# Middle stage of a fused vision-tower kernel: the order of the parts of a step rewritten on TensorE, ScalarE, VectorE and SyncE

## What is computed

```python
h = tokens(x)
h = h + attn_L0(layernorm(h))       # distances to 256 fixed positions, softmax
h = h + ffn_L0(layernorm(h))        # matmul with fp8-quantised operands
h = h + attn_L1(layernorm(h))       # softmax(h h^T / sqrt(512)) h within an image
h = h + moe_L1(layernorm(h))        # top 6 of 64 experts + shared experts
```

## Time and profile before

| what | us |
| --- | --- |
| median of 3 runs (4627.1 to 4649.3) | 4639.25 |
| the profiled execution, its own time | 4668.67 |
| its span, first to last instruction | 4666.8 |
| TensorE busy in the span | 2796.7 |
| VectorE busy | 2238.7 |
| ScalarE busy | 1579.3 |
| GpSimd busy | 2460.1 |

### The profile page before, as it was taken

How to read it: one execution, slowest core, us unless ns; L and a number is a source line. 1 busy time by engine, 2 the same in 40 slices (tenths; PEclk the granted TensorE clock), 3 DMA queues, 4 the chain that set the end, 5 groups by cost and what they waited for, 6 DMA issues and landing times. The chain is left out here.

```text
span 4666.8 us, 63125 instructions
## 1 busy us (share of the span) xinstructions
PE 2796.7 (60%) x14076; PEld 2117.4 (45%) x14077; DVE 2238.7 (48%) x7761; ACT 1579.3 (34%) x4281; POOL 2460.1 (53%) x2518
## 2 busy tenths in 40 slices
PE   5888856455545445455454336666666657677663
PEld 4777733233223222232232225655565556566563
DVE  6999965454434444344354333333333333365564
ACT  5777743232222222232222102222222222222221
POOL 5777713445544545435445535555555555565653
PEclk8999965555555555555555557777777776766676
DMA  7777711121221212211112123333333323377774
GB/s 268 248 246 245 245 32 57 61 66 63 67 63 58 63 60 64 65 58 62 61 62 66 61 57 92 94 90 91 84 84 81 84 81 84 106 228 242 237 236 166
DMA packets 401889, 522.45 MB, mean 112 GB/s; under 512 B 65596, under 2 KB 329490, under 8 KB 390514
## 3 DMA queue, kind: packets, MB, share of 16 engines
q1 hardware_dynamic: 318546, 373.60, 26.7%
q0 software_dynamic: 83232, 147.75, 9.3%
HBM read 257.02 MB, written 264.08 MB: 112 GB/s over the span
## 5 line engine op out<-in xcount | busy, mean ns | idle before, releaser
L1089 POOL DMA_INDIRECT xed<-xr,idxs x1014 | 985.9, 972 | 1098.6 <-DVE xr L1671 802.4
L1098 POOL DMA_INDIRECT ytk<-yo,idxy x1080 | 1050.8, 973 | 843.7 <-issue 792.7
L1348 PE MATMUL wide<-wdt,hT 64*128 x2160 | 469.3, 382 | 584.1 <-DVE hT L1839 558.0
L1348 PEld LDWEIGHTS wide<-wdt,hT 64*128 64x128 f32 x2160 | 402.0, 276 | 637.1 <-issue 632.2
L1830 DVE SCALAR_TENSOR_TENSOR ae<-the,bank 128x256 f32<-128x256 f32 x270 | 113.6, 421 | 800.5 <-ACT the L1479 787.7
L1263 PE MATMUL wide<-xn,e 128*128 128x128 f32 (+3 forms) x1024 | 274.9, 392 | 261.9 <-ACT e L1416 247.3
L1488 ACT ACTIVATE yo<-wide,gi 128x128 f32<-128x128 f32 x1080 | 307.3, 370 | 334.1 <-PE wide L1348 183.1
L1330 PE MATMUL bank<-wgu,xeT 128*128 x2160 | 405.4, 350 | 20.2 <-issue 11.3
L1330 PEld LDWEIGHTS bank<-wgu,xeT 128*128 128x128 f32 x2160 | 385.6, 268 | 27.8 <-issue 27.2
L1263 PEld LDWEIGHTS wide<-xn,e 128*128 128x128 f32 (+3 forms) x1024 | 156.9, 202 | 378.2 <-ACT e L1416 261.0
L1473 ACT ACTIVATE xeT<-bank 128x512 f32<-128x512 f32 x270 | 164.4, 609 | 457.2 <-remote 262.6
(11 more groups left out here) (331 smaller groups left out, 5251.8 us busy)
## 6 DMA issues: line engine op xcount, KB each, us to landing
xin<-xed SPq DMA_DIRECT2D x1080, 74.0 KB
ytk<-zeros SPq DMA_DIRECT2D x42, 1536.0 KB, 9.6
yg<-ytk SPq DMA_DIRECT2D x42, 1536.0 KB
xs<-in_xcol SPq DMA_DIRECT2D x42, 1280.0 KB, 6.7
ytk<-yo,idxy POOLq DMA_INDIRECT x1080
xed<-xr,idxs POOLq DMA_INDIRECT x1014
H<-in_ximg SPq DMA_DIRECT2D x4, 2704.0 KB, 22.2
h1d<-H SPq DMA_DIRECT2D x42, 256.0 KB, 9.5
```

The costliest lines, as they stand in the source:

```text
L1089: p.indirect_dma_start(xed[:, :], bass.IndirectOffsetOnAxis(ap=idxs[:, slot, j, k:k + 1], axis=0), xr[:, slot, j, :], None).then_inc(scat[ ...
L1098: p.indirect_dma_start(ytk[:, :], bass.IndirectOffsetOnAxis(ap=idxy[:, slot, j:j + 1], axis=0), yo[:, slot % ES, j, :], None)\
L1348: last = pe.matmul(eO[slot % 2][:, j * D:(j + 1) * D], hT[:, slot % 2, j, :], wdt[:, bass.ds(e, 1), :].rearrange("p o f -> p (o f)"), star ...
```

## The change

Nothing is computed differently. The lists of parts on four engines are put in another order, some lags are changed, two parts are split in two, two table loads are written out, and the waits are adapted to the new order.

```diff
-    LATE = 5
+    LATE = 4
...
-            braid(sp, 2, place_of(GR + 2, LATE) + 1, LATE,
-                  [('b', 0, load_h1), ('b', 2, load_weights), ('b', 3, store_h3), ('r', 3, halves(store_h4)), ('r', 0, load_h3)], 0, GR)
+            braid(sp, 1, place_of(GR + 2, LATE) + 1, LATE, [
+                ('b', -1, load_h1), ('b', 2, load_weights), ('b', 2, store_h3), ('r', 0, load_h3),
+                ('r', 3, halves(store_h4))], 0, GR)
...
             def turn_q(g, slot, rnd):
                 pe.wait_ge(n["xqb_r"], g + 1)
                 after(pe, n["xqT_r"], g)
+                after(pe, n["xnT_r"], g - 1)
...
             def turn_x(g, slot, rnd):
                 pe.wait_ge(n["xn_r"], g + 1)
                 after(pe, n["xnT_r"], g)
+                pe.wait_ge(n["xqT_r"], min(g + 2, NB) if isinstance(g, int) else g + 2)
+                after(pe, n["e_r"], 2 * g)
...
+            def shared_gate(g, slot, rnd):
+                nj = tiles_of(g)
+                pe.wait_ge(n["x4T_r"], g + 1)
                 after(pe, n["hs_r"], g)
+                pe.wait_ge(n["s_ws"], 64)
                 pe.matmul(rC[:, 0:nj * 128], sgu[:, 0:2 * F], x4T[:, 0:nj, :].rearrange("p j d -> p (j d)"),
...
-            parts = [('r', 1, halves(shared_up)), ('b', 0, turn_q), ('b', 0, ffn), ('b', 1, turn_x),
-                               ('b', 1, scores), ('r', 1, halves(count)), ('r', 1, halves(shared_down)), ('b', 1, mix),
-                               ('r', 0, turn_r), ('r', 0, halves(route))]
+            parts = [
+                ('r', 1, halves(shared_gate)), ('b', 0, turn_q), ('b', 2, mix), ('r', 1, halves(count)),
+                ('r', 1, halves(shared_up)), ('b', 1, turn_x), ('b', 0, ffn), ('r', 1, halves(shared_down)),
+                ('b', 1, scores), ('r', 0, turn_r), ('r', 0, halves(route))]
...
+            def ready_sqrt(g, slot, rnd):
+                a.nop(nofuse=True)
+                a.preload_act_table(ACT.Sqrt)
...
-            braid(a, 0, WHOLE[1], LATE, [('r', 1, halves(tanh)), ('b', 0, norm_q), ('b', 1, root_x), ('r', 0, root_r), ('b', 0, copy_q),
-                              ('b', 1, copy_x), ('r', 1, probs), ('b', 1, expo), ('r', 0, halves(copy_x4))], 0, GR)
+            norm_q(0, 0, 0)
+            braid(a, 0, WHOLE[1], LATE, [
+                ('b', 2, expo), ('r', 1, halves(tanh)), ('r', 1, probs), ('r', 1, ready_sqrt), ('b', 1, root_x),
+                ('b', 0, copy_q), ('b', -1, norm_q), ('b', 1, copy_x), ('r', 0, root_r), ('r', 0, ready_exp),
+                ('r', 0, halves(copy_x4))], 0, GR)
...
+            def stats_x(g, slot, rnd):
                 v.wait_ge(n["h2_r"], g + 1)
+                after(v, n["xn_r"], g)
                 stats(h2[:, slot, :, :], bstc, mvc, 4, "bnc", "mvc_r", g)
...
-            order = [('b', 1, ffn_out), ('r', 1, halves(silu_gate)), ('b', 0, quant), ('r', 0, stats_r), ('b', 1, root_x),
-                     ('r', 0, root_r), ('b', 1, norm_x), ('b', 2, attn_out), ('r', 1, choose), ('r', 1, halves(silu_up)),
-                     ('r', 1, place), ('r', 1, denominator), ('r', 0, norm), ('r', 1, shared_out)]
+            order = [
+                ('b', 0, quant), ('r', 1, choose), ('r', 1, choices), ('b', 1, ffn_out), ('b', 1, stats_x),
+                ('r', 1, halves(silu_gate)), ('b', 1, root_x), ('b', 1, norm_x), ('b', 2, attn_out),
+                ('r', 1, place), ('r', 1, halves(silu_up)), ('r', 1, denominator), ('r', 0, stats_r),
+                ('r', 1, shared_out), ('r', 0, root_r), ('r', 0, norm)]
```

More of the change, by code:

```diff
@@ L1124, in load_h3 @@
                 nj = tiles_of(g)
-                last = 3 * (slot // 2) + 2 + slot % 2
+                exact = isinstance(g, int)
+                last = min((TG * 128 * g + TG * 128 - 1) // (2 * T), NB - 1) if exact else 3 * (slot // 2) + 2 + slot % 2
                 for p in range(2):
-                    stored = 3 * rnd + (last - p) // 2 + 1
-                    sp.wait_ge(h3_out[p], 32 * (min(stored, NB // 2) if isinstance(stored, int) else stored))
+                    stored = (0 if exact else 3 * rnd) + (last - p) // 2 + 1
+                    after(sp, h3_out[p], 32 * stored)
                 after(sp, n["h4_r"], g - 3)
@@ L1436, in root_x, with ready_exp @@
                 a.activation(sdb[:, :], mvc[:, :, 1], ACT.Sqrt, bias=c["eps_ln"][:, :]).then_inc(n["sdb_r"], 1)
+            def ready_sqrt(g, slot, rnd):
+                a.nop(nofuse=True)
+                a.preload_act_table(ACT.Sqrt)
+            def ready_exp(g, slot, rnd):
+                a.nop(nofuse=True)
+                a.preload_act_table(ACT.Exp)
             def root_r(g, slot, rnd):
@@ L1533, in ffn_out @@
                 after(v, n["h3_r"], g - 1)
-                after(v, n["xn_r"], g)
                 v.scalar_tensor_tensor(h2[:, slot, :, :], pF[:, :].rearrange("p (j d) -> p j d", j=4),
                                        fscale[:, 1:2], h1s[:, slot, :, :], ALU.mult, ALU.add).then_inc(n["h2_r"], 1)
+            def stats_x(g, slot, rnd):
                 v.wait_ge(n["h2_r"], g + 1)
+                after(v, n["xn_r"], g)
                 stats(h2[:, slot, :, :], bstc, mvc, 4, "bnc", "mvc_r", g)
@@ L1605, in choose, with choices @@
                                 top1[:, slot % 2, 0:nj].unsqueeze(2).to_broadcast([128, nj, TOPK]), ALU.add).then_inc(n["d6_r"], 1)
+            def choices(g, slot, rnd):
+                nj = tiles_of(g)
                 v.wait_ge(n["rep_r"], g + 1)
```

## The result

The changed kernel takes 4585.0 us in the median (4574.3 to 4594.7, four runs), the kernel before, run beside it, 4634.7 us: ratio 0.9888, 95% interval 0.9854 to 0.9923, 50 us less. A second set of runs gave 4592.9 against 4633.3 us, 0.9924 (0.9895 to 0.9953). It is faster, as forecast, but by 50 us where the forecast gain was 141 us.

The account below looks back on a forecast made before the run. The middle stage was taken as a burst-to-burst chain, not bound by any full engine. Terms -101, -24, -13 and -3 made -141 us: profile 4528, median 4498 us; range 4440 to 4525, with handovers to 4560.

Parts of the forecast that it names:

- the lock: Later part of every scatter burst: increments arrive late or only at its end, about 33.4 (one-step) or 34.2 us in.
- 4 written-out pairs: Interval pairs in the stretch ahead of the loops: 86.1 us each against 92.1, -24 us together.
- 14 pairs in loops: Middle stage, one one-step plus one two-step interval each: 7.2 us less per pair, -101 us together.
- last five intervals: End of the middle stage, mostly r parts: -3 us.
- the two waits named: Two-step interval: VectorE's waits for exponentials and tanh (1.8 us) and for the counts (2.96 us) go.
- one-step interval: Burst start to next burst with one step between: 40.2 us against 40.9; 38.5 if half of `place`'s handovers pass.
- the much faster rival: `place` passes ahead of the lock, bursts follow at 31 to 34 us: -300 us, 4340 us; chance 0.12.
- the slower rival: The lock begins earlier, before some 14 us, catching work ahead of `place`: +67 us, 4706 us; chance 0.14.
- two-step interval: Burst start to next burst with two steps between: 50.0 us against 56.5, bounds 48.6 to 51.4.
- half of `quant`: Two-step interval: 1.4 of `quant`'s 2.8 us is left behind the lock, the rest passes ahead.
- The head: Stretch ahead of the first burst: `LATE = 4` starts r groups one step earlier, -13 us.
- The small price: Scatters slowed by VectorE: 0.2 us more on each of 1014 would take back the whole gain; chance 3 in 100.

Follow-up runs that it names:

- The paused burst: Changed kernel with GpSimd waiting behind a burst's twelfth scatter until those twelve have landed; one execution 4344.5 us, 0.947 of before's 4587 us.
- place ahead of attn_out: Changed kernel with count ahead of mix on TensorE, place and denominator ahead of silu_gate, second layernorm and attn_out on VectorE; 4553.7 us, ratio 0.983.
- count ahead of scores: Kernel before with only those two entries of TensorE's list exchanged; 4585.7 against 4587.5 us, ratio 1.0003.
- a fulfilled wait: Changed kernel with a long-fulfilled wait behind a burst's twelfth scatter; 3452 us in one execution and 3462 in a second try, where nothing was held.
- GpSimd's own work: Changed kernel with a 2 us iota on GpSimd behind a burst's twelfth scatter; 3550 us and, second try, 3552 us, where nothing was held.

## Why the prediction was right in direction and wrong in size

Two steps failed. In the chain, the lock was taken to begin 16 us into a one-step burst, so that `attn_out` would be done ahead of it; it begins earlier, and `attn_out` waited for its end. And the profile's distance from the median was carried over as a constant. Where the 141 us went, from the profiled executions (before with 1126.1, 2492.2 and 2695.3 us from the same timeline, after 724.1, 1087.2, 2385.8 and 2596.3 us):

| stretch | forecast | before | after | moved |
| --- | --- | --- | --- | --- |
| to the first burst | -13 | 757.6 | 724.1 | -33.5 |
| 4 written-out pairs | -24 | 368.5 | 363.1 | -5.4 |
| 14 pairs in loops | -101 | 1366.1 | 1298.6 | -67.5 |
| last five intervals | -3 | 203.1 | 210.5 | +7.4 |
| the rest | 0 | 1973.3 | 1978.0 | +4.7 |
| profile | -141 | 4668.7 | 4574.3 | -94 |
| timed median | -141 | 4634.7 | 4585.0 | -50 |

**The mechanism** held in its outline: the stage is a chain from burst to burst, an interval is the time to the lock's end and what is left behind it, and the two waits named (exponentials first behind the lock, `slotm` for the counts) went. That TensorE's own instructions go slowly inside a burst was not part of it. `quant` doesn't wait behind the h1 load: it waited for xq three times, 14.8 us in all, and never behind the first burst. `place` didn't pass ahead of the lock in the changed kernel, where the shortest one-step interval took 40.4 us, so the much faster rival falls too. The paused burst's 4344.5 us are near that rival's 4340 by chance: they are 243 us below before on their chip, where the rival gave 300.

**The one-step interval (40.2 forecast, 41.5 measured)** was the step of the chain that failed. It counted `attn_out` among what is done "to some 16 us", ahead of the lock, because the first late increment of before came 16.2 us in. That was the first one that anyone waited for in that interval, not the first that was held. The trace holds the answer: it records when a semaphore is updated, and each increment can be set beside its record. In before none of 159 increments in the first 8 us of a burst was late; of 34 between 8 and 10 us six were over 1 us late, and of 44 between 10 and 12 us 15 were, by up to 12.4 us. In the changed kernel the increments of `mix` in one-step bursts, issued 11.4 to 14.1 us in, were seen at 33.5 to 34.4 us. In the interval shown, 7.3 us stood behind the lock instead of 6.8, and its end came at 34.1, not 33.4: 41.5 us against 40.9 before, where 40.2 had been forecast. That is the milder form of the slower rival, which I had put at an onset before 14 us.

**The two-step interval (50.0, measured 51.3 in the mean)** is two cases. `attn_out` of the step without r parts was left out of the sum (1.3 us), and "half of `quant`" was wholly behind the lock in eight or nine of 14 (another 1.4): 50.0 + 2.7 = 52.7 against 52.3. Where `mix` came earlier, 48.2 to 50.0.

**The written-out pairs and the tail.** In the written-out steps of before the lock had ended earlier, and I let the new order keep that (46 us for two-step); it took 49.8. In the tail, LATE = 4 keeps b parts beside one more burst: the second of the last five intervals took 52.4 us, before 46.4. With LATE = 5 the last five take 202.7 us, as before, so the 7.4 us are LATE's.

**The head** gave more than forecast. LATE gives 13.2 us in the profiles (736.7 to 723.5), as worked out. The new order alone shortens it about as much again (110.0 us from the first write of xqb to the first burst in the second profile of before, 97.9 with LATE = 5): I had set this at nothing. The other 8 us are no effect of the order: the first write of xqb comes at 638.2 us instead of 646.3. They arise in the first stage, whose program is the same. Before and after:

```profile
51.21 14.95 POOL L592 TENSOR_TENSOR weff<-w,gam 128x384 f32<-128x384 f32 x22
57.17 9.84 DVE L787 TENSOR_SCALAR xh<-H,mv,rs 128x128 f32<-128x128 f32 x4 [0.60 <-ACT rs L708]
67.07 1.11 PE L638 MATMUL bank<-ident,xh 128*128 128x128 f32 x4 [6.59 <-DVE xh L787]
```

```profile
51.29 9.54 POOL L592 TENSOR_TENSOR weff<-w,gam 128x384 f32<-128x384 f32 x14
57.63 4.06 DVE L787 TENSOR_SCALAR xh<-H,mv,rs 128x128 f32<-128x128 f32 x4 [0.61 <-ACT rs L708]
```

In before GpSimd runs 22 products in a row where it runs 14 after, and four operations of VectorE last until about the end of these, 9.84 us instead of 4.06. TensorE stands 6.59 us for them, and its granted clock then falls to 0.50, the lower of its two levels (1.2 GHz), from 65 to 75 us, where it is 1.00 (2.4 GHz) after. In all 20 profiles, the four with 9.3 us or more for these operations are the four whose first xqb comes at 646 to 647 us; in the 16 others they take 2.5 to 4.7 us and it comes at 636 to 639 us. Both orders are among the slow and among the fast ones, so it is no effect of the change.

**Scatters beside VectorE.** The reading that a scatter takes 0.96 us "while VectorE works or stands" was too simple. The earlier trace rows themselves have 1.31, 1.03 and 1.05 us, and in the whole trace of before 104 scatters took over 1 us, each beside VectorE's work, up to 1.48 us. So the trace did show it. The small price was right: 11 us in all.

**From the profile to the median.** I moved the profiled execution's 29.4 us over unchanged. With increments held, that offset isn't a constant: against the median of its other executions it is +33 us for before, -11 to -16 for the changed kernel, +4 for it with LATE = 5, +14 for place ahead of attn_out, +15 for count ahead of scores. This took back 44 of the 94 us, as much as all errors in the chain (141 - 94 = 47). Where nothing is held the profile and the timed runs agree within 3 us for both kernels. What a profiled execution does to the held increments was not found out, so which intervals are shorter in a timed run of before stays open too.

**Not known when forecasting:** the lock is no property of the kernel. The same program takes 4633 or 3518 us, and every order that I priced was priced in the held condition. That pauses open it is seen in one kernel in one execution; whether a fulfilled wait or GpSimd's own work would do so was not tested where it matters.

## What to carry over

When a wait is removed, list what stands next in each in-order queue and ask of each whether its input was ever waited for before: an increment that nobody waited for has an unknown time of arrival, and it may be the next wait. A late time seen in a wait is an upper bound for when lateness begins; the trace's records of semaphore updates give it without anyone waiting. Take a profile of before twice and compare it with its timed runs before you carry a difference of profiles over to a median. And compare a profile of an edit with a profile of before from the same chip.

## What the runs showed of the hardware that was not expected

The same kernel, before, with the same instructions, ran at 4587 to 4639 us and at 3516 to 3520 us. In the first condition increments of TensorE and VectorE that fall into a burst of GpSimd's indirect DMAs were up to 23 us late in the changed kernel (12 us in before); all were recorded at most 4.3 us after the burst's end, and none of ScalarE's was late in either kernel. In the second condition none of the 1807 (before) and 1844 (changed) increments in the loops was over 0.5 us late. The transfers aren't slower: a packet of the scatters' queue took 77 ns in the mean held and 76 ns not held (before, 750 to 2000 us). The trace itself differs too: held, it lacks a fifth of the update records (1433 of 1807 in before), not held it has all 1807.

It touches the last stage too: from the last full burst of the changed kernel on it takes 1978.0 us held and 1459.3 us not. SyncE shows it as well. Before, held, one h1 load took 0.70 us in its queue and the next came 3.5 us later; not held the next came 1.3 us later:

```profile
1560.75 1.09 SPq L1111 DMA_DIRECT2D h1s<-h1d  x1
1562.03 0.25 SPq L1112 DMA_DIRECT2D h1s<-h1d  x1
```

Of SyncE's register instructions between 750 and 2000 us 133 of 482 took over 0.5 us held, none of 673 not held.

A gap in the middle of a burst (2.9 us in the burst shown) let increments through and was worth 5% of before in one execution where they are held, of which the new order gives some 1%. Where they are not held it cost 1.2 to 1.5% of before, and 3.3% of the changed kernel. What causes the condition is not known, and before a run nothing here tells it. The change of this case is faster in both, by 0.8 to 1.1% and by 2.0%.
